# Tokens' tables and first octets fetched by the tower's program; first relus by halves, y products pair by pair

## The reference

```python
# tower: x (32, 64, 64, 1) -> h (32, 64, 64)
v = transpose(concat([x, gx, gy]) @ p_w + p_b)          # 32 channels
for i in range(4):
    x_ft = rfft2(v)                                     # only 12 + 12 rows and 12 columns of modes are kept
    x1 = irfft2(modes mixed over channels with fw1, fw2)
    v = x1 + einsum('bcxy,cd->bdxy', v, w_w[i]) + w_b[i]
    v = (v - mean) * rsqrt(var + 1e-5) * bn_g[i] + bn_b[i]   # mean, var over batch, x, y
    if i < 3: v = relu(v)
h = einsum('bcxy,cu->bxyu', v, q_w) + q_b
# tokens: every image row h[b, x, :] is a token of 64 features
h = layernorm(h + attention_tower(h))     # 4 layers: linear attention over the 64 tokens of an image, MLP with gelu
h = layernorm(h + mixture(h))             # shared MLP + the best 2 of 4 experts
```

## Time and profile before

| | us |
|---|---|
| median of 3 runs | 772.47 (770.98 to 776.26) |
| the profiled execution's own time | 773.5 |
| its span, first to last instruction | 771.7 |
| mean granted clock of TensorE | 0.907 |
| busy: PE / DVE / ACT | 626.0 / 546.1 / 362.3 |

### The profile page before, as it was taken

One profiled execution on the slowest core, in us unless ns is written; L12 is line 12 of the kernel. 1 busy time (PEld: TensorE's weight loads), 2 busy tenths in 40 slices (PEclk: granted clock), 3 DMA queues, 4 the chain that ended last, 5 costly groups with the idle time before them and its releaser, 6 DMA issues. The chain is left out here.

```text
span 771.7 us, 25833 instructions
## 1 busy us (share of the span) xinstructions
PE 626.0 (81%) x11935; PEld 434.3 (56%) x11935; DVE 546.1 (71%) x810; ACT 362.3 (47%) x517; POOL 71.1 (9%) x126
## 2 busy tenths in 40 slices
PE   5989974766899955766999937888776999999997
PEld 3967751323877742334877723332532888777754
DVE  4568887994567878994488889987741768667363
ACT  0034459600035459500044565737221688888763
POOL 3100000002100000003000000002000223233200
PEclk9599997998599987998699969999978999999999
DMA  9200000005100000006000000013003300000001
GB/s 348 101 3 3 4 23 1 1 2 200 50 3 3 3 2 1 2 1 247 4 3 3 3 8 2 2 42 137 6 8 95 112 2 2 1 3 2 2 0 29
DMA packets 13925, 28.15 MB, mean 36 GB/s; under 512 B 5613, under 2 KB 6125, under 8 KB 13689
## 3 DMA queue, kind: packets, MB, share of 16 engines
q1 hardware_dynamic: 13528, 25.77, 9.5%
q10 hardware_dynamic: 288, 0.73, 0.3%
HBM read 25.44 MB, written 1.05 MB: 34 GB/s over the span
## 5 line engine op out<-in xcount | busy, mean ns | idle before, releaser
L461 ACT ACTIVATE V<-ps,wts 128x1024 f32<-128x1024 f32 x96 | 101.8, 1111 | 260.3 <-PE ps L926 260.3
L592 DVE BATCH_NORM_STATS2 stats<-V 128x6 f32<-128x512 f32 x192 | 117.7, 677 | 24.5 <-ACT V L461 24.5
L926 PE MATMUL ps<-tab,A 64*128 64x128 f32 x1536 | 105.2, 283 | 13.6 <-ACT V L461 7.8
L926 PEld LDWEIGHTS ps<-tab,A 64*128 64x128 f32 x1536 | 91.9, 189 | 37.3 <-issue 22.2
L534 DVE STREAM_TRANSPOSE A<-V 128x2048 f32<-128x2048 f32 x48 | 107.4, 2278 | 6.2 <-ACT V L440 6.2
L801 PE MATMUL ps<-A,tab 128*128 128x384 f32 x192 | 75.1, 539 | 32.7 <-DVE A L541 32.7
L440 ACT ACTIVATE V<-V,small 128x2048 f32<-128x2048 f32 x48 | 96.2, 2084 | 3.8 <-DVE small L639 3.8
L789 PE MATMUL ps<-A,tab 32*32 32x512 f32 x1536 | 60.5, 648 | 35.4 <-DVE A L534 35.4
L801 PEld LDWEIGHTS ps<-A,tab 128*128 128x128 f32 x192 | 37.4, 204 | 79.1 <-DVE A L541 59.8
L583 DVE STREAM_TRANSPOSE A<-ps 128x2048 f32<-128x2048 f32 (+1 forms) x27 | 55.4, 2071 | 25.9 <-PE ps L913 25.9
L541 DVE STREAM_TRANSPOSE A<-ps 128x1024 f32<-128x1024 f32 x48 | 56.6, 1219 | 10.9 <-PE ps L789 10.9
(11 more groups left out here) (257 smaller groups left out, 857.3 us busy)
## 6 DMA issues: line engine op xcount, KB each, us to landing
A<-in_modes SPq DMA_DIRECT2D x32, 384.0 KB, 7.1
r_ky<-in_modes SPq DMA_DIRECT2D x16, 384.0 KB, 5.6
wl<-in_layers SPq DMA_DIRECT2D x3, 452.0 KB, 5.4
V<-in_pixels SPq DMA_DIRECT2D x1, 1024.0 KB, 12.8
wm<-in_mixture SPq DMA_DIRECT2D x1, 874.5 KB, 7.7
tab<-in_table SPq DMA_DIRECT2D x1, 656.5 KB
A<-in_turned SPq DMA_DIRECT2D x1, 512.0 KB
tower_out<-A SPq DMA_DIRECT2D x4, 128.0 KB, 2.3
```

Source lines behind the costliest of these rows:

```text
L461: nc.scalar.activation(Vm[:, 2 * h:2 * h + 2, r, 512 * q:512 * (q + 1)], bank(half_of_u(q, r) + 2 * h, 2).rearrange("p (m n) -> p m n", m= ...
L592: last = nc.vector.bn_stats(stats[:, 16 * q + 4 * r + m, :], Vm[:, m, r, 512 * q:512 * (q + 1)])
L926: last = nc.tensor.matmul(ps[:, at:at + P], G[(2 * q + quad) % 4][rows, x:x + P], inv_y[rows, :], start=step < 2 and quad == 0, stop=step ...
```

## The change

1. **The seam.** `r_ky` is no longer freed between the programs. A table of 256 columns (unit matrix and reordering matrix) is taken out of the tokens' constants and put behind the tower's table. SP loads it into `r_ky` once the products into `flat` are done, then loads octet 0 behind the store of octet 1 and octet 1 behind the store of octet 2, into `r_ky` too. Each store has a semaphore of its own. SP no longer waits for the last stores in the tower: the tokens' program loads octets 2 and 3 when their own stores are in. PE opens the tokens' program with a wait for that table and octet 0, and waits for `cst` only before it centres. Six semaphores become three (`s_step`, `s_stepa`, `s_stepv`) with the same meaning.
2. **The heads of layers 1 to 3.** Relus 0 and 1 and turns 0 and 1 are made in two halves of 8 chunks, each turn half waiting for its relu half.
3. **The y products** of u = 0 and u = 7 are made pair by pair: 32 products over 256 columns once the first pair is turned, and 32 more once the second is.

```diff
+                if q == 1:
+                    sp.wait_ge(s_step, 1)
+                    sp.dma_start(r_ky[:, 0:N_TURN], table[:, T_TURN:T_DRAM]).then_inc(s_tokens[0], 16)
                 sp.wait_ge(s_ua, 2 * (q + 1))
                 sp.wait_ge(s_uv, 2 * (q + 1))
                 sp.dma_start(tower_out..., A[...]).then_inc(s_out[q], 16)
-            sp.wait_ge(s_out, 16 * OCT)
+                if q in (1, 2):
+                    sp.wait_ge(s_out[q - 1], 16)
+                    for b2 in range(2):
+                        sp.dma_start(token_room(r_ky, q - 1, b2), token_rows(tower_out, q - 1, b2)).then_inc(s_tokens[q - 1], 16)
...
             def relu(n):
-                pair = Vk[:, :, P * n:P * (n + 1)]
-                nc.scalar.activation(pair, pair, ACT.Relu, bias=bias, scale=scale).then_inc(s_relu, 1)
+                for k in range(0, 16, 8 if n < 2 else 16):
+                    pair = Vk[:, k:k + 8 if n < 2 else 16, P * n:P * (n + 1)]
+                    nc.scalar.activation(pair, pair, ACT.Relu, bias=bias, scale=scale).then_inc(s_relu_half if n < 2 and k == 0 else s_relu, 1)
...
                 def turn(n):
+                    if n < 2:
+                        dve.wait_ge(s_relu_half, 2 * (l - 1) + n + 1)
+                        nc.vector.transpose(T[n % 3]...[:, 0:8], Vk[:, 0:8, P * n:P * (n + 1)])
...
+                def forward_y_by_pairs(u):
+                    at_least(pe, s_Y, PAIRS * (l - 1) + 2 * u)
+                    for p in range(2):
+                        pe.wait_ge(s_T, PAIRS * (l - 1) + 2 * u + p + 1)
+                        slot, place = (2 * u + p) % 3, 1 - p if u % 3 == 1 else p
+                        ...   # 32 products over 256 columns
+                    last.then_inc(s_fy, 1)
...
-                    forward_y(0)
+                    forward_y_by_pairs(0)
                     for u in range(FU):
                         forward_x(u, 0)
                         forward_x(u, 1)
-                        if u + 1 < FU:
+                        if u + 2 < FU:
                             forward_y(u + 1)
+                        elif u + 1 < FU:
+                            forward_y_by_pairs(u + 1)
...
-            for g in range(G):
+            for g in (2, 3):
+                sp.wait_ge(s_stored[g], 16)
                 for b2 in range(2):
-                    sp.dma_start(part(u0, g)..., rows).then_inc(s_u[g], 16)
+                    sp.dma_start(token_room(room, g, b2), token_rows(tower_out, g, b2)).then_inc(s_u[g], 16)
...
-            pe.wait_ge(s_cst, 16)
+            pe.wait_ge(s_u[0], 48)
             for g in range(G):
                 for t in range(GP):
-                    nc.tensor.matmul(bank(g, 0, P * t, P), part(spec, g)[...], ident, start=t == 0, stop=False)
-                pe.wait_ge(s_u[g], 32)
+                    nc.tensor.matmul(bank(g, 0, P * t, P), part(spec, g)[...], turn, start=t == 0, stop=False)
+                if g:
+                    pe.wait_ge(s_u[g], 32)
...
+            pe.wait_ge(s_cst, 16)
             for g in range(G):
                 pe.wait_ge(s_uraw, g + 1)
                 nc.tensor.matmul(bank(g, 1), centre, part(h0T, g), start=True, stop=True).then_inc(s_ucen, 1)
```

More of the change, by code:

```diff
@@ L76, in last_layer_tables @@
     last_x[:, 0:2 * MODES, 1] = -np.sin(two_pi * np.outer(kx, y))
-    return [t.reshape(P, -1) for t in (weigh, twice, gather, last_y, last_x)]
+    in_order = np.kron(np.eye(2), np.kron(np.eye(16)[:, np.arange(16).reshape(4, 4).T.ravel()], np.eye(4)))
+    return [t.reshape(P, -1) for t in (weigh, twice, gather, last_y, last_x, np.eye(P), in_order)]
 def constants():
@@ L222, in tower_kernel @@
     KEPT["spec"] = spec
+    r_ky = nc.alloc_sbuf_tensor("r_ky", [P, RING * MODES * 2 * CH], f32)
+    s_out = [nc.alloc_semaphore(f"s_out{q}") for q in range(OCT)]
+    s_tokens = [nc.alloc_semaphore(f"s_tokens{q}") for q in range(OCT)]
+    KEPT["room"], KEPT["s_out"], KEPT["s_tokens"] = r_ky, s_out, s_tokens
     with ExitStack() as ctx:
@@ L312, in tower_kernel @@
         s_relu = sem("s_relu")
+        s_relu_half = sem("s_relu_half")
         s_T = sem("s_T")
@@ L533, in turn @@
                         dve.wait_ge(s_fy, FU * (l - 1) + (n - 3) // 2 + 1)
-                    nc.vector.transpose(T[n % 3].rearrange("p (k n) -> p k n", k=16), Vk[:, :, P * n:P * (n + 1)]).then_inc(s_T, 1)
+                    rest = 8 if n < 2 else 0
+                    nc.vector.transpose(T[n % 3].rearrange("p (k n) -> p k n", k=16)[:, rest:], Vk[:, rest:, P * n:P * (n + 1)]).then_inc(s_T, 1)
                 def spectra_y(u, p):
@@ L778, in _ @@
                 layout = l % 2
+                def forward_y_by_pairs(u):
[3 more added lines that the diff above has]
+                        slot, place = (2 * u + p) % 3, 1 - p if u % 3 == 1 else p
+                        for yh in range(2):
+                            for j in range(4):
+                                for i in range(4):
+                                    rows = slice(Q * i, Q * (i + 1))
+                                    out = bank(i)[Q * j:Q * (j + 1), 256 * place:256 * (place + 1)]
+                                    last = nc.tensor.matmul(out.rearrange("p (k c) -> p k c", k=8), fwd_y[rows, Q * yh:Q * (yh + 1)],
+                                                            T3[rows, j // 2, yh, slot, 8 * (j % 2):8 * (j % 2) + 8, :],
+                                                            start=yh == 0, stop=yh == 1, tile_position=(Q * i, Q * j))
+                    last.then_inc(s_fy, 1)
                 def forward_y(u):
@@ L1121, in token_kernel @@
     NX = TILES * EMB
-    spec = KEPT["spec"]
+    spec, room, s_stored, s_u = (KEPT[k] for k in ("spec", "room", "s_out", "s_tokens"))
     with ExitStack() as ctx:
@@ L1150, in token_kernel @@
         wm = sb("wm", [P, E_ALL])
-        cst = sb("cst", [P, 4 * P + 2 + EXPERTS])
+        cst = sb("cst", [P, 3 * P + 2 + EXPERTS])
         dev = sb("dev", [P, TILES])
@@ L1163, in token_kernel @@
         mean, prefer = cst[:, 3 * P:3 * P + 2], cst[:, 3 * P + 2:3 * P + 2 + EXPERTS]
-        in_order = cst[:, 3 * P + 2 + EXPERTS:]
+        turn, in_order, u0 = room[:, 0:P], room[:, P:2 * P], room[:, N_TURN:N_TURN + NX]
         def bank(g, i, at=0, n=GW):
@@ L1174, in stat @@
             return st[:, i, GT * g:GT * (g + 1)]
-        s_u = [sem(f"s_tokens{g}") for g in range(GROUPS)]
         s_wl = [sem(f"s_wl{l}") for l in range(DEPTH)]
@@ L1631, in _ @@
         def _(pe):
-            pe.wait_ge(s_cst, 16)
+            pe.wait_ge(s_u[0], 48)
             for g in range(G):
                 for t in range(GP):
-                    nc.tensor.matmul(bank(g, 0, P * t, P), part(spec, g)[:, P * t:P * (t + 1)], ident, start=t == 0, stop=False)
-                pe.wait_ge(s_u[g], 32)
+                    nc.tensor.matmul(bank(g, 0, P * t, P), part(spec, g)[:, P * t:P * (t + 1)], turn, start=t == 0, stop=False)
+                if g:
+                    pe.wait_ge(s_u[g], 32)
                 for t in range(GP):
```

58 lines of the change are left out of this document (28 added, 30 removed).

## The result

| | median us | runs | ratio to before, 95% interval |
|---|---|---|---|
| before | 772.47 (766.49 to 776.26) | 19 | |
| changed | 766.27 (761.37 to 769.75) | 19 | 0.9923 [0.9902, 0.9944] |

The change makes the kernel 6.0 us faster (4.3 to 7.6). I had forecast 12.5, with 757 as the lower end and 766 as the upper. Single executions now and then run at a lower clock over their whole length and take some per cent longer: the ratios leave them out, and of the profiled execution of e15, which was one, no time is read.

What follows compares the result with a forecast made beforehand. No engine is full; a sequence of stages, each with its own limit, bounds the kernel. Heads 7.8, tails 0.65 and seam 4.6 sum to 13.05 us off 773.5, giving 760.45, adjusted to 760.0; range 757 to 766.

Steps and rivals of the forecast that it cites:

- Heads: Starts of layers 1 to 3: half relus and turns bring spectra_y earlier, 7.8 us together, bounds 6.6 and 8.4.
- later relus move 0.1 to 0.2 us back on ACT, which cost nothing, since relu 3 is done: Heads: the delay of later relus is free, relu 3 being done by about 124.5 and due after 126.7.
- Tails: Last y product of layers 1 to 3, pair by pair: +0.65 us gained, of it 0.25 in layer 3; bounds -1.4 and +2.5.
- Behind the tails: Mode loads and mixing after the last y product: nothing gained or lost, layer 1's 3.89 us stall stays as long.
- Seam: Between the two programs: centring comes 6.1 us earlier, less 1.5 for a low clock, so 4.6 us gained.
- The 3.9 us for a load of octet 3: Seam: time from issue to landing of octet 3's second DMA, taken between the median 3.3 and 4.5 us.
- The last four products (0.65 us) and centring: Seam: after octet 3 lands at 594.7, four products remain and centring starts from about 595.35, instead of 601.45.
- the 1.5 us that I took off: Seam: cost of centring and what follows coming into a low clock, at half the clock about 1.5 us.
- (a): Rival: clock and transfers move against the change in layers 1 to 3, 2 us a layer, 766 us; chance 0.13.
- (b): Rival at the seam: the early fetch does little, worth 2 us instead of 4.6, total 763; chance 0.13.
- (c): Rival: code stalls of about 3.9 us open in each head or tail, 772 us, no change; chance 0.07.
- (d): Rival in the loops: clock not granted to products by pairs, TensorE becomes the bound, about 791 us; chance 0.03.

Runs made afterwards that it cites:

- e15: Changed kernel with TensorE's code behind the head of layer 1 moved by 96 pairs of empty products: 760.2 us, ratio 0.9826 to before.
- e7: Changed kernel with relu 2 and turn 2 also made by halves: 761.6 us, ratio 0.9872 to before.
- e1: Seam as in the changed kernel, forward parts as in the kernel before: 771.2 us, ratio 1.0001 to before.
- e13: Changed kernel with TensorE's code behind the head of layer 1 moved by 128 pairs of empty products: 766.6 us, ratio 0.9905 to before.
- e8: Changed kernel with the tokens' constants and first layer's weights also fetched early by the tower's program: 763.6 us, ratio 0.9898 to before.
- e5: Changed kernel with 64 pairs of empty products put in TensorE's list before the head of layer 1: 759.4 us, ratio 0.9858 to before.
- e4: Changed kernel run again with nothing edited: 765.5 us, ratio 0.9937 to before.

## Why the prediction was wrong, point by point

- **Heads: right mechanism, size off.** I said 7.8 us; measured 1.99 + 1.93 + 1.64 = 5.56. The step that failed is the one on the relus: "later relus move 0.1 to 0.2 us back on ACT, which cost nothing, since relu 3 is done". I checked relus 1 and 3 and left out relu 2, which turn 2 needs first: it waited 0.69 us, and e7 takes the wait away. My own terms said so: relu 2 done at 116.19 + 4 x 1.06 + 2.0 = 122.43, turn 2 due at 122.12. The first turn starts 1.35 us behind the relu, where I had 1.17, since half a relu takes 1.14 us ((14.56 - 5 x 2.0) / 4) and not 1.06. The four half turns took 4.62 us, not 4.76. That makes 0.18 + 0.69 - 0.14 = 0.73 us a layer, and 2.2 in the three. The y products took 4.54 us at the low clock, not 1.94 twice and a gap (4.32), and end before turn 2 does.
- **Tails: right where the trace can tell.** Layer 3 gained 0.22 of the 0.25 forecast. What layers 1 and 2 gained cannot be told from the clock's dips: loop and tail took 53.67 and 52.40 us instead of 53.89 twice, but in e1, whose tails are as before, 53.90 and 52.17.
- **Behind the tails: right, and beside the point.** The stall stayed (3.89 to 3.71 in its load rows, 3.78 to 3.59 in the products). I saw it, took it for code, and counted the 128 pairs that are added, but did not ask what another number would do: moving the code by 64 pairs is worth 5 to 7 us in the changed kernel.
- **Seam: mis-sized, 4.6 forecast, 2.4 in its stretch, and nothing to be seen when alone.** The barrier's wait went nearly as said (1.5 us of 1.7), and TensorE started at once. The 3.9 us for a load of octet 3 was right too (3.7). The step that failed is what I put behind it, "The last four products (0.65 us) and centring": I had TensorE wait for octet 3 alone, at full clock. It waited for octet 2, whose second load took 5.4 us, and had three blocks of four products left, at 1.2 GHz: 2.72 us instead of 0.65, though I expected a low clock there myself. So centring came 10.02 us behind the last eviction, not 7.62: 2.1 us from these products, 0.3 from the later start of the program and the wait. Of the 2.1, 1.3 are the clock and 0.8 the two more blocks (e7 needs 1.44 us for the three at full clock). For how far the low clock would reach behind the centring I had no row, and none of before shows the 1.5 us that I took off; the changed kernel's trace shows 1.3 in the centring and what follows, e7 and e13 none. With the clock up, as there, the same seam gains 5.0 us, so the 4.6 was in reach, by luck of the clock. Of octet 2's 6.0 us, 1.9 go with the loads of `cst` and `wl` (e8, one trace), and 1.1 with the place of TensorE's code (e5 and the traces like it). The fixed cost of about 2.0 us a DMA that the Trainium skill ("DMA: Bandwidth & Descriptors", "Anatomy of one DMA") gives, with which the seam would have made 6.5, was further off than my 3.9; that section fits it to DMAs issued by GpSimd, and these are SyncE's.
- **The rivals.** What came is (a) and (b), each in part. (a): the clock fell against the change at the seam, 2.6 us. That the dips of layers 1 and 2 fell at one place says nothing on how their moment is set; that the same kernel's first norm came at 117.76 and at 121.08 us says more. (b): octet 2 took 6.0 us. (c), stalls in the heads, did not open: TensorE's first y product waits for VectorE, not for "issue". (d) did not come, though its sign did, the first products over x of each layer at 1.2 GHz (5.49, 4.38 and 4.49 us): from the second on they took 2.85 us, at full clock.
- **The sum.** Heads 5.6, tail of layer 3 0.2, seam 2.4, less the 0.9 of the tokens' part, is 7.3, within the measured 4.3 to 7.6. Heads and seam, each 2.2 us short of the forecast, are most of what it was off by. The two parts alone gave 4.2 and 0.0, less than their stages; whether more than noise and the clock is in that stays open.

## What to carry to other kernels

Check each operand of a shortened chain, in order, against the engine that makes it; here the one that was skipped was the late one. A row named "issue" in the middle of equal products was the sign here that the place of TensorE's code counts: before judging an edit there, move the code behind it by half a block with empty products in an idle stretch, and compare both kernels in both places. Before you give a cause to a stage's time, look for the same stage in the other traces: the seam took 15.7 to 18.6 us with one and the same code. A transfer that is fetched early should take its neighbours along: beside the late ones octet 2 took 6.0 us to be usable, without them 4.1.

## What was not expected of the hardware

- 64 pairs of empty products gave the changed kernel 5.0 us by the ratios (6.9 by the medians) and the kernel before 3.6, and 128 pairs nothing beyond the noise.
- Octet 2, two loads of 64 KB, was usable 4.1 us after the tokens' program started when no other loads of the program were under way (e8), 4.9 beside 650 KB of them (e5), and 6.0 beside them with TensorE's code at another place.
- The same code up to the first norm took 116.15, 117.76 and 121.08 us in three executions; between 37 and 53 us the granted clock was 0.97, 0.86 and 0.79.
- The wait of TensorE for octet 2 cost 2.6 us more than its length where the granted clock stayed low behind it (changed kernel, e4), and nothing more in e7 and e13, with the same seam.
